# Cross attention of block one: scores from two 64-row halves of PE, the shift row laid by SP's transfers, the low key parts stacked by GpSimd

## The chip, the cores and the metric

The kernel runs on one core of one Trainium2 chip. The metric is the time of one execution on the device, in microseconds (us), less is better. The core has five engines that run side by side and wait for one another by semaphores: PE (TensorE, matrix products, with its weight loads listed apart as PEld), DVE (VectorE), ACT (ScalarE), POOL (GpSimd) and SP (SyncE, which here only issues transfers, DMAs). Products go to PSUM, of eight banks of 512 f32 columns by 128 partitions; everything else lies in SBUF, of 128 partitions.

## The reference

A chain of four attention blocks over x of 32 batches by 56 tokens by 128 channels, with a context of 1500 rows for each batch. The change is in the cross attention of block one:

```python
def _L1_xattn_ref(x, context, Wqkv, bqkv, Wos, bos, Wq, bq, Wkv, bkv, Woc, boc, W1, b1, W2, b2):
    ...
    h = _ln(x)
    q = (h @ Wq + bq).reshape(Bx, Nx, H, D)          # 16 heads of 8 channels
    kv = (context @ Wkv + bkv).reshape(Bx, Mx, 2, H, D)
    k, v = (kv[:, :, 0], kv[:, :, 1])
    a = _sdpa(q, k, v).reshape(Bx, Nx, C)            # softmax(q k / sqrt(8)) v
    x = x + (a @ Woc + boc)
```

## The kernel before, in words

The kernel goes through its stages one after the other. The stage of the change is `cross_attention` (L998), behind `tokens_l1_cross` (L926), which makes its queries. It handles one batch a step, with the engines on different batches at a time: a batch's keys are projected in one step, the maxima of its scores are sought in the next, its scores and weighted sums are made in the two after that.

What a batch goes through:

- PE projects keys (`project_k`, L1145, three products of 500 columns in f32) and values (`project_v`, L1158), ACT copies them out of PSUM (L1246, L1256, L1258).
- POOL splits the f32 keys `kf` into an f16 high part `kh` (L1101) and an f16 low part `kl` (L1103), so that scores from f16 products keep their precision.
- `piece` (L1168) makes rough scores from the high parts, 21 products of 128 by 500 in f16, and DVE takes the maximum of each (L1289). The maximum of each query is the shift of its softmax. DVE collects them (`top`, L1310), PE turns them from a column to rows (L1218), DVE copies the 7 rows of 128 to `topt` (L1300), and POOL's `lay_shift` (L1110) spreads them over rows 96 to 102 of `qs`.
- SP stacks the keys by DMA (L1066, L1070): in `ks`, for each of four groups of four heads, rows 0 to 31 and 32 to 63 hold the high part, 64 to 95 the low part, and rows 96 to 102 hold ones. `qs` holds the queries' high part, low part and high part against them (made by POOL, L1087, from `qst`), each masked to its head, and the shift at the ones. So one product of 103 rows gives the exact score less its shift.
- `score` (L1183): for each of 12 slices of 125 keys, four such products (one for a group of heads), 128 weight columns of `ks` and 224 moving columns of `qs`. They fill two PSUM banks of `stp`; ACT takes the exponential of both at once (L1235).
- `weigh` (L1200): the weighted sums, f32, on four parts of PE of 32 columns each (`tile_position=(0, q)`), three slices at a time, four times in a batch.

The order of PE's work is written out by hand in `step` (L1207 on): 12 slots of a step, in each a weighing, a projection or the turning of the shift where one is due, then `piece`, `score`, `piece`. Slots 7, 10, 1 and 4 have the weighings; the turning is in slot 11. The score of slot 2 is the first of a batch, and is where PE waits for the stacked keys, the spread queries and the shift. The score's place is always between two other products of full size.

Before the stage, `tokens_l1_cross` makes `qst` from copies of the query weights (`wqs`, three times 32 columns for each group), and ACT (L975) and DVE (L960) split it into parts. Row products on parts of PE also occur elsewhere: `norm_pe` (L452) and L1389 use four parts of 32 rows (`tile_position=(32 * c, 0)`). All transfers of SP go in the order in which it issues them, and a semaphore counts 16 for each that has landed.

## Time and profile before

| | |
|---|---|
| median of 3 runs | 2227.27 us (2222.23 to 2234.25) |
| the profiled execution | 2220.8 us, its span 2219.0 us |
| PE busy in the span | 1897.6 us (86%) |
| DVE, ACT, POOL busy | 1490.4, 1396.4, 955.3 us |
| mean granted clock of PE | 0.917 of 2.4 GHz |
| stage of the change, first score to the last | 464.7 to 1139.5 us |

The page gives sums by engine and by line; the stage is read from stretches of the span (busy time of each engine in it), from the list of who waited for whom, and from the timeline, which gives each instruction or run of like instructions with its start and length. A product's listed length holds some 0.165 us in which its results are still on their way while the next already streams: a product of 500 columns is listed with 0.37 us and the next starts 0.21 us after it. So the distance from start to start is the time that a product costs PE.

### The profile page before, as it was taken

The page shows a single profiled execution, that of the slowest core. Times are in us where ns is not written, and L with a number is a line of the kernel's source. Part 1 is how long each engine was busy: PE and PEld are TensorE (multiplying, and loading weights), DVE is VectorE, ACT ScalarE, POOL GpSimd, SP SyncE. Part 2 cuts the span into 40 slices and gives each one's busy share as a digit, 9 for nine tenths or more (in the row PEclk, how much of TensorE's full clock was granted, in tenths as well). Part 3 has the DMA queues.
Part 4 walks back from the last instruction along what each step waited for, and adds up shares of the span by engine and source line. Part 5 has one row for each costly group of instructions (what it writes and reads, how often), then busy time and mean ns, then how long its engine had stood idle before and what let it go on. Part 6 is the DMA issues. An engine that isn't in the chain of part 4 may idle for free. (4 is left out here: it accounts for less than half of the span.)

```text
span 2219.0 us, 57559 instructions
## 1 busy us (share of the span) xinstructions
PE 1897.6 (86%) x19877; PEld 1284.0 (58%) x19877; DVE 1490.4 (67%) x2708; ACT 1396.4 (63%) x2431; POOL 955.3 (43%) x1151
## 2 busy tenths in 40 slices
PE   4888676789999999999988887656899999999988
PEld 3888333256666666666653555233466666666653
DVE  3688578666666666666632332697488888888883
ACT  3787233356666666666633334433799999999963
POOL 0000064244454544545400000251688888888840
PEclk9899778799999999999988889755899999999989
DMA  7788100133332333333230997000011111111100
GB/s 210 222 257 257 17 1 0 42 78 96 90 94 83 90 90 84 98 88 90 72 103 20 272 290 222 0 0 28 29 46 52 43 42 42 42 42 42 42 1 17
DMA packets 64286, 190.38 MB, mean 86 GB/s; under 512 B 19886, under 2 KB 27294, under 8 KB 64222
## 3 DMA queue, kind: packets, MB, share of 16 engines
q1 hardware_dynamic: 59614, 164.95, 26.5%
q0 software_dynamic: 4608, 24.58, 2.8%
q8 instruction: 39, 0.64, 0.1%
q14 instruction: 25, 0.20, 0.0%
HBM read 127.13 MB, written 25.49 MB: 69 GB/s over the span
## 5 line engine op out<-in xcount | busy, mean ns | idle before, releaser
L1289 DVE TENSOR_REDUCE c_part<-c_mxp 128x1 f32<-128x500 f32 x672 | 429.0, 678 | 207.9 <-PE c_mxp L1168 207.7
L1235 ACT ACTIVATE c_e<-c_stp 125x896 f32<-125x896 f32 x384 | 349.4, 917 | 167.6 <-PE c_stp L1183 166.4
L1936 ACT ACTIVATE c_e<-c_sp,alpha 128x750 f32<-128x750 f32 x448 | 393.0, 896 | 16.9 <-PE c_sp L1881 16.9
L1168 PE MATMUL c_mxp<-c_kh,c_qb 128*128 128x500 f16 x672 | 254.4, 381 | 11.1 <-DVE c_part L1289 6.9
L1958 DVE TENSOR_SCALAR c_pt<-c_tp 125x768 bf16<-125x768 f16 x448 | 245.6, 550 | 2.1 <-PE c_tp L1894 0.8
L1894 PE MATMUL c_tp<-ident_h,c_ph 128*128 128x128 f16 x2688 | 224.3, 220 | 19.0 <-DVE c_pt L1958 15.8
L1894 PEld LDWEIGHTS c_tp<-ident_h,c_ph 128*128 128x128 f16 x2688 | 178.0, 98 | 106.1 <-DVE c_pt L1958 60.3
L1972 DVE TENSOR_SCALAR c_ph<-c_e,c_inv 128x1500 f16<-128x1500 f32 x224 | 231.2, 1032 | 0.1
L1881 PE MATMUL c_sp<-c_ki,c_qb 128*128 128x375 bf16 x896 | 218.7, 326 | 10.5 <-ACT c_e L1936 10.0
L1183 PE MATMUL c_stp<-c_qs,c_ks 103*128 103x224 f16 x1536 | 210.2, 259 | 2.5 <-ACT c_e L1235 2.5
L1183 PEld LDWEIGHTS c_stp<-c_qs,c_ks 103*128 103x128 f16 x1536 | 147.2, 98 | 72.1 <-issue 20.5
L1110 POOL TENSOR_TENSOR c_qs<-c_topt,mask_tile_ 7x896 f16<-7x896 f32 x32 | 53.8, 1681 | 293.8 <-DVE c_topt L1300 293.8
L1200 PE MATMUL c_pvp<-c_e,c_vx 125*32 125x168 f32 (+1 forms) x6144 | 173.8, 261 | 1.0 <-ACT c_e L1235 1.0
L1200 PEld LDWEIGHTS c_pvp<-c_e,c_vx 125*32 125x32 f32 x6144 | 145.1, 110 | 48.4 <-issue 33.6
L1947 ACT ACTIVATE c_rounded<-c_pp,round,rdelta 128x500 f32<-128x500 f32 (+1 forms) x192 | 149.6, 779 | 36.3 <-PE c_pp L1870 22.3
L1824 POOL TENSOR_SCALAR c_clamped<-c_rounded 128x500 f32<-128x500 f32 (+1 forms) x192 | 136.9, 713 | 36.4 <-ACT c_rounded L1947 16.3
L1833 POOL TENSOR_SCALAR c_ki<-c_clamped 128x500 bf16<-128x500 f32 x96 | 113.4, 1181 | 17.3 <-issue 15.8
L1881 PEld LDWEIGHTS c_sp<-c_ki,c_qb 128*128 128x128 bf16 x896 | 69.0, 98 | 83.6 <-ACT c_e L1936 46.7
L1103 POOL TENSOR_TENSOR c_kl<-c_kf,c_kh 128x500 f16<-128x500 f32 x96 | 109.1, 1136 | 8.0
L1870 PE MATMUL c_pp<-a2wv,c_ct 128*125 128x128 f32 x768 | 107.6, 284 | 2.6 <-ACT c_rounded L1947 2.6
L1865 PE MATMUL c_pp<-c_ct,a2wk 128*128 128x500 f32 x192 | 105.4, 632 | 4.9 <-POOL c_ph L1815 2.9
L1145 PE MATMUL c_pp<-c_ct,wkv 128*128 128x500 f32 x192 | 104.5, 627 | 4.8 <-PEq L87 2.2
(276 smaller groups left out, 3534.7 us busy)
## 6 DMA issues: line engine op xcount, KB each, us to landing
c_ct<-ctx_turned SPq DMA_DIRECT2D x64, 750.0 KB
ctx_turned<-l_ct POOLq DMA_DIRECT2D x32, 750.0 KB, 7.6
c_ks<-c_kh SPq DMA_DIRECT2D x256, 93.8 KB
f_ct<-ctx_turned SPq DMA_DIRECT2D x32, 750.0 KB
l_cn<-in_ctx SPq DMA_DIRECT2D x32, 672.0 KB
f_cn<-in_ctx SPq DMA_DIRECT2D x32, 672.0 KB
c_ks<-c_kl SPq DMA_DIRECT2D x128, 93.8 KB
l_cn<-in_ctx SPq DMA_DIRECT2D x32, 78.0 KB
```

What stands on the lines that cost most here:

```text
L1168: pe.matmul(mxp[:, (PIECES * p + s) % 2, 0:500], qh[p][:, 128 * (s // 3):128 * (s // 3) + 128], kh[p][:, 500 * (s % 3):500 * (s % 3) + 500 ...
L1183: last = pe.matmul(stp[:, 2 * (j % 2) + g // 2, 224 * (g % 2):224 * (g % 2) + 224], ks[p][:, g, KP * j:KP * j + 128], qs[p][:, 224 * g:224 ...
L1200: last = pe.matmul(pvp[q:q + 32, c:c + width], vx[p][:, j, g, :], e[:, j % (2 * GROUP), NQ * h:NQ * h + width], start=(j == 0 and g < 4), ...
L1235: act.activation(e[:, j % (2 * GROUP), :].rearrange("p (a c) -> p a c", a=2), stp[0:KP, 2 * (j % 2):2 * (j % 2) + 2, 0:448], ACT.Exp, scal ...
L1289: dve.reduce_max(part[:, s // 3, s % 3:s % 3 + 1], mxp[:, (PIECES * p + s) % 2, 0:500], axis=AX.X).then_inc(piece_max, 1)
L1824: pool.tensor_scalar(clamped[k % 2][0:rows, 0:width], rounded[k % 2][0:rows, 0:width], ROUND + 127.0, ROUND - 128.0, ALU.min, ALU.max).the ...
L1881: last = pe.matmul(sp_[:, 2 * h + k, 0:375], qb[p][:, 128 * t:128 * t + 128], ki[p][:, HALF * h + 375 * k:HALF * h + 375 * k + 375], start ...
L1894: last = pe.transpose(tp[:, h, 128 * k:128 * k + 128], ph[t % E_BUFFERS][:, KP * j:KP * j + 128], m.ident_h[:, :])
L1936: act.activation(e[t % E_BUFFERS][:, HALF * h:HALF * h + HALF] .rearrange("p (k c) -> p k c", k=2), sp_[:, 2 * h:2 * h + 2, 0:375], ACT.Ex ...
L1947: act.activation(rounded[k % 2][0:rows, 0:width], pp[0:rows, 0:width], ACT.Identity, bias=m.round[0:rows, 0:1], scale=m.rdelta[0:rows, d:d ...
L1958: dve.tensor_scalar(pt[p][:, 6 * h:6 * h + 6, 128 * t:128 * t + 128], tp[0:KP, h, 0:6 * 128].rearrange("p (j c) -> p j c", j=6), HALF_ROUN ...
L1972: dve.tensor_scalar(ph[t % E_BUFFERS][:, 0:NK], e[t % E_BUFFERS][:, :], inv[:, t:t + 1], HALF_ROUND, ALU.mult, ALU.add).then_inc(p_ready, 1)
```

## The change

The score's product of 103 rows becomes two of 64 rows, on the upper and the lower half of PE's rows, each with half of the heads and 112 moving columns; the two halves write different PSUM banks. Within a half, rows 0 to 15 and 16 to 31 hold the high part of two heads' keys, row 32 is a row of ones for the shift (rows 33 to 47 are ones as well, against zeros), and rows 48 to 63 hold the low part. `ks` is filled by 16 transfers of 16 rows from SP and 8 of 16 rows from POOL (before: 12 of 32 rows from SP). The shift goes to rows 32 and 96 of `qs` by 8 small transfers from SP in place of POOL's instruction L1110. POOL's four instructions L1087 become one on 128 rows by 448 columns. `qst` is laid out for it, with weights from 12 small loads in place of 6 and products of 128 columns in place of 96. The memsets of ones cover 128 partitions, and SP and POOL wait for them before the first stacking.

```diff
-    for t in range(3):
-        loads.append((m.wqs[:, :, 32 * t:32 * t + 32], w["L1_xattn_Wq"].rearrange("c (g r) -> c g r", g=4)))
-        loads.append((m.bqs[32 * t:32 * t + 32, :], w["L1_xattn_bq"].rearrange("(g r) -> r g", g=4)))
+    for half in range(2):
+        wide, narrow = w["L1_xattn_Wq"][:, 64 * half:64 * half + 64], w["L1_xattn_bq"][64 * half:64 * half + 64]
+        for at in (0, 16, 48):
+            a = 64 * half + at
+            loads.append((m.wqs[:, :, a:a + 16], wide.rearrange("c (g r) -> c g r", g=4)))
+            loads.append((m.bqs[a:a + 16, :], narrow.rearrange("(g r) -> r g", g=4)))
...
-                        dve.scalar_tensor_tensor(out=m.qst[32:64, g, cols(c)], in0=bank[32:64, 4 + i % 4, 0:CH],
-                                                 scalar=m.bqs[32:64, g:g + 1], in1=m.qst[32:64, g, cols(c)],
+                        dve.scalar_tensor_tensor(out=m.qst[:, g, cols(c)], in0=bank[:, 4 + i % 4, 0:CH],
+                                                 scalar=m.bqs[:, g:g + 1], in1=m.qst[:, g, cols(c)],
                                                  op0=ALU.add, op1=ALU.subtract).then_inc(qs_low, 1)
...
-                        act.activation(m.qst[:, g, cols(c)], bank[0:96, 4 + i % 4, 0:CH], ACT.Identity,
-                                       bias=m.bqs[:, g:g + 1]).then_inc(qs_high, 1)
+                        act.activation(m.qst[:, g, cols(c)], bank[:, 4 + i % 4, 0:CH], ACT.Identity,
+                                       bias=m.bqm[:, g:g + 1], scale=m.mask_rows[:, 2:3]).then_inc(qs_high, 1)
...
-        ks = pair("ks", [96 + NT, 4, W], F16)
+        ks = pair("ks", [128, 4, W], F16)
-        qs = pair("qs", [96 + NT, HQ], F16)
+        qs = pair("qs", [128, HQ // 2], F16)
...
+                        sp.wait_ge(qs_spread, n - 1)
+                        sp.wait_ge(top_copied, n - 1)
+                        for t in range(NT):
+                            for c in (0, 64):
+                                at = 128 * t + c
+                                row, at = (32, at) if at < HQ // 2 else (96, at - HQ // 2)
+                                if t == NT // 2:
+                                    sp.dma_start(qs[p][row:row + 1, at:at + 64], topt[t:t + 1, c:c + 64]
+                                                 ).then_inc(shift_sent[p], 16)
+                                elif c == 0:
+                                    sp.dma_start(qs[p][row:row + 1, at:at + 128], topt[t:t + 1, :]
+                                                 ).then_inc(shift_sent[p], 16)
                     if live(1):
                         r = 1 - p
+                        if not live(2):
+                            sp.wait_ge(ones_set, 2)
                         if live(3):
                             wait_apart(sp, scored, NJ * (n - 2), beat)
                         sp.wait_ge(k_high, 3 * n)
-                        for t in range(2):
-                            for g in range(4):
-                                sp.dma_start(ks[r][32 * t:32 * t + 32, g, 0:NK], kh[r][32 * g:32 * g + 32, 0:NK]
-                                             ).then_inc(stacked[r], 16)
-                        sp.wait_ge(k_low, 3 * n)
-                        for g in range(4):
-                            sp.dma_start(ks[r][64:96, g, 0:NK], kl[r][32 * g:32 * g + 32, 0:NK]
-                                         ).then_inc(stacked[r], 16)
-                sweep(sp, step, 1)
+                        for at in (0, 16):
+                            for half in (0, 64):
+                                for g in range(4):
+                                    sp.dma_start(ks[r][half + at:half + at + 16, g, 0:NK],
+                                                 kh[r][half + 16 * g:half + 16 * g + 16, 0:NK]
+                                                 ).then_inc(stacked[r], 16)
+                sweep(sp, step, 2)
...
-                    for g in range(4):
-                        last = pool.tensor_tensor(
-                            qs[p][0:96, 4 * NQ * g:4 * NQ * (g + 1)].rearrange("p (h q) -> p h q", h=4),
-                            m.qst[:, g, tokens(a)].rearrange("p (o q) -> p o q", o=1).to_broadcast([96, 4, NQ]),
-                            m.mask_quad[0:96, :].rearrange("p (h o) -> p h o", o=1).to_broadcast([96, 4, NQ]),
-                            ALU.mult)
-                    last.then_inc(qs_spread, 1)
+                    pool.tensor_tensor(qs[p][:, :].rearrange("p (g h q) -> p g h q", g=4, h=2),
+                                       m.qst[:, :, tokens(a)].rearrange("p g (o q) -> p g o q", o=1)
+                                       .to_broadcast([128, 4, 2, NQ]),
+                                       m.mask_rows[:, 0:2].rearrange("p (o h u) -> p o h u", o=1, u=1)
+                                       .to_broadcast([128, 4, 2, NQ]), ALU.mult).then_inc(qs_spread, 1)
+
+                def stack_low(a, p, live):
+
+                    if not live(2):
+                        pool.wait_ge(ones_set, 2)
+                    wait_apart(pool, k_low, 3 * a + 3, beat)
+                    for half in (0, 64):
+                        for g in range(4):
+                            pool.dma_start(ks[p][half + 48:half + 64, g, 0:NK],
+                                           kl[p][half + 16 * g:half + 16 * g + 16, 0:NK]).then_inc(low_stacked[p], 16)
 
...
-                def lay_shift(a, p, more):
-
-                    if more:
-                        pool.wait_ge(k_low, 3 * a + 6)
-                    pool.wait_ge(top_copied, a + 1)
-                    pool.tensor_tensor(qs[p][96:96 + NT, :].rearrange("p (t c) -> p t c", t=NT),
-                                       topt[:, :].rearrange("p (o c) -> p o c", o=1).to_broadcast([NT, NT, 128]),
-                                       m.mask_tile[:, :].rearrange("p (t o) -> p t o", o=1)
-                                       .to_broadcast([NT, NT, 128]), ALU.mult).then_inc(shift_laid, 1)
-
                 def step(n, p, live):
                     if live(1):
                         spread_queries(n - 1, 1 - p, live)
+                        stack_low(n - 1, 1 - p, live)
                     if live(0):
                         if live(2):
-                            pool.wait_ge(shift_laid, n - 1)
...
-                        pe.wait_ge(stacked[p], transfers(a, p, 12))
+                        pe.wait_ge(stacked[p], transfers(a, p, 16))
+                        pe.wait_ge(low_stacked[p], transfers(a, p, 8))
                         pe.wait_ge(qs_spread, a + 1)
-                        pe.wait_ge(shift_laid, a + 1)
+                        pe.wait_ge(shift_sent[p], transfers(a, p, 8))
                     if j >= 2 or not first:
                         pe.wait_ge(exped, NJ * a + j - 1)
                     for g in range(4):
-                        last = pe.matmul(stp[:, 2 * (j % 2) + g // 2, 224 * (g % 2):224 * (g % 2) + 224],
-                                         ks[p][:, g, KP * j:KP * j + 128], qs[p][:, 224 * g:224 * g + 224],
-                                         start=True, stop=True)
+                        for half in range(2):
+                            r = 64 * half
+                            last = pe.matmul(stp[:, 2 * (j % 2) + half, 112 * g:112 * g + 112],
+                                             ks[p][r:r + 64, g, KP * j:KP * j + 128],
+                                             qs[p][r:r + 64, 112 * g:112 * g + 112], start=True, stop=True,
+                                             tile_position=(r, 0))
...
-                    dve.memset(ks[p][96:96 + NT, :, :], 1.0).then_inc(ones_set, 1)
+                    dve.memset(ks[p][:, :, :], 1.0).then_inc(ones_set, 1)
...
-                                dve.wait_ge(shift_laid, n - 1)
+                                dve.wait_ge(shift_sent[p], transfers(n - 2, p, 8))
```

## Rows read from the trace of the kernel before

**Rows 1.** Stretch: us, busy (count) of PE, PEld, DVE, ACT, POOL; PEclk, DMA share, GB/s.

```profile
464.70:1139.50 674.80, 651.15 (x9232) 460.30 (x9231) 446.67 (x802) 467.21 (x660) 319.38 (x361) 1.00 0.32 85
```

**Rows 2.** Who waited for whom between 500 and 1100 us: total, times, longest.

```profile
DVE c_part L1289 <- PE c_mxp L1168: 183.3, 280, 0.9
...
PE c_pp L1218 <- DVE c_top L1310: 16.7, 28, 0.6
```

**Rows 3.** Timeline of PE in one batch: start, us, what, count, idle before.

```profile
950.42 0.37 PE L1168 MATMUL c_mxp<-c_kh,c_qb 128*128 128x500 f16 x1
950.63 0.55 PE L1183 MATMUL c_stp<-c_qs,c_ks 103*128 103x224 f16 x4
951.02 0.38 PE L1168 MATMUL c_mxp<-c_kh,c_qb 128*128 128x500 f16 x1
951.33 1.36 PE L1200 MATMUL c_pvp<-c_e,c_vx 125*32 125x168 f32 x48
...
953.98 0.28 PE L1218 MATMUL c_pp<-ident_,c_top 128*7 128x128 f32 x1 [0.60 <-DVE c_top L1310]
954.09 0.55 PE L1183 MATMUL c_stp<-c_qs,c_ks 103*128 103x224 f16 x4
...
957.28 0.38 PE L1168 MATMUL c_mxp<-c_kh,c_qb 128*128 128x500 f16 x1
957.49 1.00 PE L1145 MATMUL c_pp<-c_ct,wkv 128*128 128x500 f32 x2
...
958.54 0.55 PE L1183 MATMUL c_stp<-c_qs,c_ks 103*128 103x224 f16 x4
```

**Rows 4.** PE's timeline, window 952.44 to 952.70, around the end of a weighing.

```profile
952.14 0.55 PE L1200 MATMUL c_pvp<-c_e,c_vx 125*32 125x168 f32 x13
952.62 0.38 PE L1168 MATMUL c_mxp<-c_kh,c_qb 128*128 128x500 f16 x1
```

**Rows 5.** As rows 1, line 1389 alone: products of 32 rows on four parts.

```profile
1151.40:1154.80 3.40, 3.38 (x16) 1.30 (x16) 0.50 1.04 373
```

**Rows 6.** As rows 1, line 445 alone: products of 128 rows, same columns.

```profile
250.20:256.40 6.20, 6.08 (x8) 2.52 (x8) 0.53 0.24 2
```

**Rows 7.** PE's timeline at 1701.6: six transposes, a weight load each.

```profile
1701.68 0.50 PE L1894 MATMUL c_tp<-ident_h,c_ph 128*128 128x128 f16 x6
```

**Rows 8.** Weight loads of the scores by line: busy us, mean ns, idle before.

```profile
L1183 PEld LDWEIGHTS c_stp<-c_qs,c_ks 103*128 103x128 f16 x1343 | 129.1, 98 | 61.8 <-issue 18.0 <-ACT c_e L1235 9.0
```

**Rows 9.** Timeline of all engines around the shift and the next batch's keys.

```profile
954.29 0.28 DVE L1300 COPY c_topt<-c_pp 7x128 f32<-7x128 f32 x1 [0.37 <-PE c_pp L1218]
...
954.72 1.68 POOL L1110 TENSOR_TENSOR c_qs<-c_topt,mask_tile_ 7x896 f16<-7x896 f32 x1 [9.08 <-DVE c_topt L1300]
...
957.54 4.94 SPq L1066 DMA_DIRECT2D c_ks<-c_kh  x8
957.61 2.11 POOL L1087 TENSOR_TENSOR c_qs<-qst,mask_quad_ 96x224 f16<-96x224 f32 x4 [1.21 <-PE c_stp L1183]
...
962.52 2.50 SPq L1070 DMA_DIRECT2D c_ks<-c_kl  x4
...
965.82 1.13 POOL L1103 TENSOR_TENSOR c_kl<-c_kf,c_kh 128x500 f16<-128x500 f32 x1
```

**Rows 10.** Timeline of SP's queue from 237.7 us: small transfers.

```profile
237.74 0.30 SPq L503 DMA_DIRECT2D wocb<-in_L_xattn_Woc  x1
238.08 0.29 SPq L503 DMA_DIRECT2D bvb<-in_L_xattn_bkv  x1
```

**Rows 11.** DMA busy tenths in 40 slices of 0.325 us, 957 to 970 us.

```profile
DMA  0000083929191929393939383848000000000000
```

**Rows 12.** GpSimd's DMA instructions, line 314: min/median/max ns, first and last start.

```profile
L314 POOL DMA_DIRECT2D ctx_turned<-l_ct x32: 533/533/749, 29.7 to 220.5; - x32
```

**Rows 13.** Timeline of DVE and PE at the stage's start.

```profile
436.29 5.07 DVE L1270 MEMSET c_ks<- 7x6016 f16 x1 [1.20 <-issue]
...
465.14 0.77 PE L1183 MATMUL c_stp<-c_qs,c_ks 103*128 103x224 f16 x3
```

More of the change, by code:

```diff
@@ L209, in _ @@
             def _(pool):
-                for t in (m.woca, m.wocb, m.bva, m.bvb):
+                for t in (m.woca, m.wocb, m.bva, m.bvb, m.bqs):
                     pool.memset(t[:, :], 0.0)
+                pool.memset(m.wqs[:, :, :], 0.0)
                 pool.memset(m.mean[:, :], 1.0 / D)
@@ L965, in _ @@
             def _(act):
+                act.wait_ge(small, 7)
                 norm_act(act, m, n2, bank)
@@ L1076, in _ @@
                 for p in range(2):
-                    pool.memset(ks[p][0:96, :, NK:W], 0.0).then_inc(set_once, 1)
                     pool.memset(kh[p][:, NK:W], 0.0).then_inc(set_once, 1)
@@ L2215, in constants @@
     spread[:, 1] = (l[:, None] == 12 + g) & (l < DH)
+    block = r % 64 // 16
+    mask_rows = np.zeros((128, 3), np.float32)
+    for h in range(2):
+        mask_rows[:, h] = (r % 16 // DH == h) & (block != 2)
+    mask_rows[:, 2] = block == 1
     key, of_head = np.arange(2 * NQ), np.arange(D) // DH
```

30 lines of the change are left out of this document (16 added, 14 removed).

## The prediction, on record before the run

> **What bounds the kernel now.** I read the busy time by stretches first. Between the first score and the last, PE is busy 651.15 of 674.80 us at the full clock (1.00), DVE 446.67, ACT 467.21, POOL 319.38 [rows 1]. The list of waits agrees: over 600 us DVE sat idle for PE's products 280 times, 183.3 us in all, while PE itself has one wait for another engine in each batch, 0.60 us for the maxima, 16.7 us in 28 batches [rows 2]. 28 batches in 600 us make 21.4 us a batch. So PE sets the pace, and whatever its queue gains or loses in a batch comes back some 32 times. The timeline shows how close its products stand [rows 3]: a product of 500 columns starts at 950.42, four score products at 950.63, the next product at 951.02. So a score costs PE 0.39 us, 4.7 us in a batch.
>
> **The score products.** With both halves streaming side by side, each half has 4 x 112 columns where the whole had 4 x 224. 0.39 us falls to some 0.19 us, worth 12 x 0.19 = 2.3 us in a batch, if nothing is added. Three things bear on it.
>
> Do row parts run side by side? Line 1389 has eight f32 products of 448 columns, 16 instructions, on four parts of 32 rows; they took 3.40 us at the half clock (0.50) [rows 5]. Line 445 has four such products on all rows, 8 instructions, and took 6.08 us at nearly the same clock (0.53) [rows 6]. Twice the work in 0.56 of the time: the parts overlap fully, so I take two halves as overlapping fully too. Their weight loads overlapped as well: 16 in 1.30 us of busy PEld [rows 5].
>
> Can the weights keep up? Each product of 112 columns brings its own load of 128 weight columns. Six transposes, each with such a load and 128 moving columns, took 0.50 us, of which the first 0.22 us is latency: 0.056 us each [rows 7]. A load is listed with 98 ns [rows 8], but most of that is latency too. So a half needs 4 x 0.047 to 4 x 0.056 us, 0.19 to 0.22; I take 0.20.
>
> What does the change of shape cost? The weighing uses PE in four parts of 32 columns. Before it the product of 500 columns starts at 951.02 and would free PE at 951.23 (its 0.21 us of streaming, as above), but the weighing starts at 951.33: 0.10 us [rows 3]. At its end, the last of its products ends at 952.14 + 0.55 = 952.69; less 0.165 us of latency its streaming ends at 952.52, and the next full product starts at 952.62: again 0.10 us [rows 4]. That is not the change of type: f16 is followed by f32 at 957.28 and 957.49 with the bare 0.21 us between [rows 3]. The trace has no switch between full and row shape with work waiting on both sides, so its cost lies between nothing and, by these rows, 0.10 us; I take 0.10, since entering and leaving the parts cost the same and f32 or f16 made no difference. Each of the 12 scores stands between two full products, so it pays twice: 0.10 + 0.01 for the first weights + 0.20 + 0.10 = 0.41 to 0.42 us against 0.39. **The switches eat the overlap**: +0.03 us x 12 = +0.36 us in a batch, 11.5 us in 32. Bounds: 0.19 us a score without any switch cost (-2.3 us in a batch), 0.45 with slow weights and both switches (+0.7).
>
> The Trainium skill (TensorEngine Tiling (Array Packing), Key Properties) says that a change of the tiling mode drains the engine; the 0.10 us in rows 3 and 4 agree for column parts, and nothing before shows it for rows. Its table of speedups on the same page gives "up to 2x" for a contraction of at most 64; by that alone the scores would save 2.3 us in a batch, 74 us in all.
>
> **The shift.** Today `topt` is ready at 954.29 + 0.28 = 954.57, POOL takes 954.72 to 956.40 [rows 9], and the score that needs it starts at 958.54 [rows 3]: 2.1 us of slack, cost zero. Now SP issues 8 transfers and they must land. SP is free then: its last instructions before are the load of the context, long issued, and it waits for this very event. Behind its wait stand the 16 stackings, which today start at 957.54 after their own wait for the scores [rows 9]; nothing is needed from them before the next batch. Small transfers were issued 0.34 us apart [rows 10], the stackings 4.94/8 = 0.62 us apart. From issue to landing: the stackings are issued from 957.54 and traffic starts at slice 5 of the DMA line, 958.6; the last is issued at some 964.4 and traffic ends in slice 29, 966.4 [rows 9, 11]. So 1.1 us to the start and 1.9 us to the end; a small one should land between 1.3 and 1.9 us after its issue. The eighth lands at 954.7 + 7 x 0.34 + 1.3 = 958.4 at best, at 954.7 + 7 x 0.62 + 1.9 = 960.9 at worst. PE needs it at 958.54 + 0.19 for three longer scores and a switch, 958.7. The wait is 0 to 2.2 us; small transfers are nearer to the pitch of rows 10, so I take 0.42 us and 1.6 us: 959.2, a wait of **0.5 us**. It holds up PE's whole queue (the next pieces, the key projections), so all of it counts: 0.5 x 31 = 15.5 us. DVE, starved by it, has slack; the one wait of PE for the maxima stays.
>
> **POOL.** It loses 1.68 us and some 1.1 us (one instruction of 448 columns in place of 2.11 us for four of 224), and gets 8 DMA instructions. The first stage shows one alone at 0.53 to 0.75 us [rows 12]. 8 x 0.57 = 4.6 us, between the spread and the next split of keys. That split now ends at 965.82 + 1.13 = 966.95 [rows 9] and moves to some 970.4; it is needed for the first piece after 954.09 + 21.4 + 0.4 = 975.9. The cover is 9 us; it would be gone at 1.25 us per instruction. Cost zero. The low parts land by some 967 and are needed at 980.
>
> **SP and DMA.** 16 x 0.62 = 9.9 us in place of 7.4, issued from 957.5 to 967.5, needed at 980; the next context load comes at 972. Same bytes. Cost zero.
>
> **Ahead of the stage.** The second memset ends at 436.29 + 5.07 = 441.4; SP now waits for it 3.8 us longer, but the first score starts only at 465.14 [rows 13]. The six more weight loads lie beside PE's work in an earlier stage. DVE, ACT and PE have as many instructions in making `qst`. Zero.
>
> **Sum.** 2220.8 us for the profiled execution + 11.5 + 15.5 = 2247.8. The median of the runs shown lies 6.5 us above that execution, so I forecast 2254 us.
>
> **Rivals.**
> - *No cost of switching to rows.* The scores save 12 x 0.18 = 2.1 us in a batch. But three of them lie between the maxima and the shift's need, which then comes 0.6 us earlier, so the wait grows to 1.1 us: 1.0 us in a batch gained, 32 us, about 2195 us; 2160 if the shift comes in time. For it: rows 5 has no gap between its parts. Against it: every entry and exit seen costs 0.10 us. It decides at 0.08 us per switch: below that the score itself gains, and below 0.06 it outweighs the wait for the shift.
> - *The shift comes in time.* Then only the switches count: 2220.8 + 11.5 + 6.5 = 2239 us. For it: the lower landing estimate.
> - *The halves don't overlap, or their weights come too slowly.* 8 x 0.05 + 0.21 = 0.61 us a score, +2.7 us in a batch, no wait for the shift: +86 us, 2313 us. Against it: rows 5 and 6, though at the half clock and in f32.
> - *Transfers or POOL's instructions slower than taken.* The wait at the upper bound, 2.2 us: +54 us more, 2305 us.
>
> **How the numbers follow.** Forecast (2240 to 2285 us) 0.50; no switch cost, or little of it 0.15; shift in time 0.14; no overlap 0.11; slow transfers 0.10. The predicted time is 2254 us. The range 2215 to 2310 leaves out most of the first rival and part of the last two. 0.5% (11 us) is about what a measurement can tell from no change: below 2216 us 0.14, between 2216 and 2238 us 0.17, above 0.69.
>
> **What would show it.** In the profile after, the two products of 500 columns around a score start 0.62 to 0.63 us apart (the 0.21 us of the first, then 0.41 to 0.42); 0.41 says that switching is free, over 0.72 that the halves take turns. The first weight load of a score starts 0.10 us after the stream before has ended. The waits list PE's scores behind SP's transfers of `qs`, once in a batch, 0.5 us each; none says in time. The stage then lasts 27 us more. DVE's idle time for PE grows; the clock stays at 1.00. I am wrong if the scores' starts are closer, if PE waits for POOL, or if another stage moves.

## The result, and the profile after

| | median, us | lowest to highest, us | runs |
|---|---|---|---|
| before | 2224.75 | 2220.31 to 2234.25 | 4 |
| after | 2306.86 | 2301.48 to 2318.10 | 4 |

The kernel is slower: ratio 1.037, 95% interval 1.0317 to 1.0422, some 82 us. The profiled execution of after is the slowest of its four: 2318.1 us, span 2316.2, 97.2 more than the span of before.

The stage by stretches, columns as in [rows 1]: the whole stage, its beginning, and its steady middle (740 to 1190 us, in which the batches take nearly the same time and the clock is 1.00).

```profile
467.80:1235.20 767.40, 660.63 (x10767) 404.40 (x10767) 454.50 (x801) 457.76 (x659) 347.82 (x479) 0.97 0.32 76
467.80:650.00 182.20, 157.18 (x2391) 93.16 (x2395) 104.91 (x182) 104.72 (x151) 83.13 (x115) 0.93 0.33 77
740.00:1190.00 450.00, 389.97 (x6384) 239.31 (x6383) 278.44 (x490) 273.64 (x397) 221.53 (x304) 1.00 0.34 80
```

The stage is 767.40 us long, where [rows 1] has 674.80: 92.6 of the 97.2 us. PE's busy time has grown by 9.5 us only, so PE stands idle. The clock column is new too: 0.97 where it was 1.00, and 0.93 up to 650 us.

Who PE waited for, over the stage, and in the last line over its steady middle, 740 to 1190 us (total, times, longest):

```profile
PE c_stp L1202 <- DMA c_qs<-c_topt: 81.5, 32, 4.8
PE c_pp L1238 <- DVE c_top L1330: 21.0, 31, 0.7
...
PE c_stp L1202 <- DMA c_qs<-c_topt: 45.5, 19, 2.6
```

One wait has come in, in each of 32 batches: the first score (line 1202) behind the shift's transfers, 45.5/19 = 2.4 us each in the middle. The wait for the maxima, PE's one wait for another engine in [rows 2], is nearly as it was: 21.0/31 = 0.68 us against 0.60.

The timeline of PE in one batch of the middle:

```profile
949.98 0.38 PE L1184 MATMUL c_mxp<-c_kh,c_qb 128*128 128x500 f16 x1
950.29 0.37 PE L1202 MATMUL c_stp<-c_qs,c_ks 64*128 64x112 f16 x8
...
952.13 0.38 PE L1184 MATMUL c_mxp<-c_kh,c_qb 128*128 128x500 f16 x1 [0.22 <-issue]
952.45 0.37 PE L1202 MATMUL c_stp<-c_qs,c_ks 64*128 64x112 f16 x8
952.75 0.38 PE L1184 MATMUL c_mxp<-c_kh,c_qb 128*128 128x500 f16 x1
...
956.04 0.37 PE L1184 MATMUL c_mxp<-c_kh,c_qb 128*128 128x500 f16 x1
958.61 0.37 PE L1202 MATMUL c_stp<-c_qs,c_ks 64*128 64x112 f16 x8 [2.20 <-DMA c_qs<-c_topt]
```

Read the distances of starts. Piece 952.13, score 952.45, piece 952.75: 0.62 us from piece to piece, where [rows 3] has 0.60. From 949.98 to 950.29 is 0.31 us, of which 0.21 us is the piece's streaming: entering the halves costs 0.10 us. Then 952.75 - 952.45 = 0.30 us: 0.20 us for eight products on two halves and 0.10 us to leave them. How the 0.30 us divide is the prediction's estimate here; the kernel with scores in pairs, below, shows it. The last piece ahead of the shift's score streams until 956.25. The score starts at 958.61, with 2.20 us of idle time ahead of it that the row puts down to the transfers.

The same batch on the other engines, DVE's copy of the maxima first:

```profile
951.65 0.28 DVE L1320 CAST c_topt<-c_pp 7x128 f16<-7x128 f32 x1 [0.37 <-PE c_pp L1238]
...
952.01 1.79 SPq L1077 DMA_DIRECT2D c_qs<-c_topt  x3
...
953.85 1.22 SPq L1074 DMA_DIRECT2D c_qs<-c_topt  x2
...
955.11 1.85 SPq L1077 DMA_DIRECT2D c_qs<-c_topt  x3
...
956.13 3.92 POOL L1118 DMA_DIRECT2D c_ks<-c_kl  x8
...
957.17 10.09 SPq L1089 DMA_DIRECT2D c_ks<-c_kh  x16
```

The eight shift transfers (lines 1077 and 1074) start 0.08 us after the copy's end at 951.93 and are issued every 0.61 to 0.63 us: 3 in 1.79 us, 2 in 1.22, 3 in 1.85. The last issue begins near 956.34; PE starts 2.3 us later, so it has landed by some 2.2 us after its start. (The profile's own time from issue to landing has a median of 1.7 us over these transfers, 3.1 at most.) [rows 9] shows GpSimd doing the same work in one instruction of 1.68 us. What followed in the queues gave no trouble: GpSimd's eight stackings took 3.92 us, SP's sixteen 10.09 us, and the list of waits has neither as a releaser of PE.

To compare kernels I use the period of a batch: the starts of DVE's copies of the maxima between 750 and 1100 us, the last less the first, divided by one less than their count. The rows give count, min/median/max ns, first and last start; the second is of before.

```profile
L1320 DVE CAST c_topt<-c_pp x15: 278/279/279, 760.8 to 1095.0; 7x128 f16<-7x128 f32 x15
```

```profile
L1300 DVE COPY c_topt<-c_pp x16: 277/279/279, 761.0 to 1083.0; 7x128 f32<-7x128 f32 x16
```

(1095.0 - 760.8)/14 = 23.87 us, against (1083.0 - 761.0)/15 = 21.47 us.

### The profile page after: what moved, and what is told of

Read it like the earlier page. It is cut to its first block and busy times, and to the rows that moved or that the text cites. A ratio compares the mean times of both kernels' runs of the same rounds, so it can differ in the third digit from the quotient of the medians.

```text
span 2316.2 us, 61141 instructions
## 1 busy us (share of the span) xinstructions
PE 1895.0 (82%) x21413; PEld 1224.6 (53%) x21413; DVE 1500.8 (65%) x2709; ACT 1390.3 (60%) x2431; POOL 991.0 (43%) x1279
## 5 line engine op out<-in xcount | busy, mean ns | idle before, releaser
L1309 DVE TENSOR_REDUCE c_part<-c_mxp 128x1 f32<-128x500 f32 x672 | 437.3, 678 | 288.3 <-PE c_mxp L1184 287.9
L1184 PE MATMUL c_mxp<-c_kh,c_qb 128*128 128x500 f16 x672 | 261.0, 391 | 11.6 <-DVE c_part L1309 6.5
L1901 PE MATMUL c_sp<-c_ki,c_qb 128*128 128x375 bf16 x896 | 218.6, 326 | 10.5 <-ACT c_e L1956 10.0
L1202 PE MATMUL c_stp<-c_qs,c_ks 64*128 64x112 f16 x3072 | 144.6, 215 | 83.7 <-DMA c_qs<-c_topt 81.5
L1202 PEld LDWEIGHTS c_stp<-c_qs,c_ks 64*128 64x128 f16 x3072 | 83.9, 96 | 215.3 <-issue 163.8
L1105 POOL TENSOR_TENSOR c_qs<-qst,mask_rows_ 128x448 f16<-128x448 f32 (+1 forms) x32 | 29.9, 934 | 356.6 <-PE c_stp L1202 356.6
L1118 POOL DMA_DIRECT2D c_ks<-c_kl x256 | 125.5, 497 | 7.6 <-issue 5.0
L1184 PEld LDWEIGHTS c_mxp<-c_kh,c_qb 128*128 128x128 f16 x672 | 65.0, 97 | 85.5 <-DVE c_part L1309 27.6
## 6 DMA issues: line engine op xcount, KB each, us to landing
c_ks<-c_kh SPq DMA_DIRECT2D x512, 46.9 KB
c_ks<-c_kl POOLq DMA_DIRECT2D x256, 46.9 KB
```

Of the source, the lines that this page charges most:

```text
L1184: pe.matmul(mxp[:, (PIECES * p + s) % 2, 0:500], qh[p][:, 128 * (s // 3):128 * (s // 3) + 128], kh[p][:, 500 * (s % 3):500 * (s % 3) + 500 ...
L1202: last = pe.matmul(stp[:, 2 * (j % 2) + half, 112 * g:112 * g + 112], ks[p][r:r + 64, g, KP * j:KP * j + 128], qs[p][r:r + 64, 112 * g:112 ...
L1309: dve.reduce_max(part[:, s // 3, s % 3:s % 3 + 1], mxp[:, (PIECES * p + s) % 2, 0:500], axis=AX.X).then_inc(piece_max, 1)
L1901: last = pe.matmul(sp_[:, 2 * h + k, 0:375], qb[p][:, 128 * t:128 * t + 128], ki[p][:, HALF * h + 375 * k:HALF * h + 375 * k + 375], start ...
```

## The experiments

| kernel | median, us | ratio to before, 95% interval | period, us |
|---|---|---|---|
| before | see below | 1 | 21.47 |
| after | 2306.9 | 1.037 (1.0317 to 1.0422) | 23.87 |
| after without the shift | 2222.3 | 1.0006 (0.999 to 1.0022) | 21.63 |
| before with halves only | 2222.5 | 1.0009 (0.9993 to 1.0025) | 21.63 |
| before with the shift by SP | 2270.5 | 1.0226 (1.0198 to 1.0253) | 22.84 |
| shift in four transfers | 2223.8 | 1.001 (0.999 to 1.0029) | 21.65 |
| eight transfers out of HBM | 2222.7 | 1.001 (0.9989 to 1.0031) | 21.64 |
| shift in two queues | 2245.3 | 1.0091 (1.0064 to 1.0118) | 21.94 |
| low stackings back on SP | 2227.6 | 1.0021 (1.0003 to 1.0038) | 21.64 |
| scores in pairs | 2212.0 | 0.9932 (0.99 to 0.9964) | 21.06 |
| pairs, key eviction earlier | 2198.4 | 0.9879 (0.9854 to 0.9904) | 20.70 |
| wait filled | 2300.3 | 1.0344 (1.031 to 1.0378) | 23.90 |

The periods are each read from one profiled execution. The kernel before had a median of 2221.35, 2223.06 and 2222.08 us beside the first four, the next four and the last two of them.

### After without the shift

```diff
-                    if live(2):
-                        sp.wait_ge(qs_spread, n - 1)
-                        sp.wait_ge(top_copied, n - 1)
-                        ...  the eight sp.dma_start(qs[p][row:row + 1, ...], topt[...])
...
-                        pe.wait_ge(shift_sent[p], transfers(a, p, 8))
```

> The kernel after without SP's eight transfers of the shift and the waits on them: the exponentials are taken without the maxima (this part of the computation is left out; the maxima are still made). Theory A (the loss is the wait for the shift, 81.5 us in the profile after, plus the switches of shape, 12 x 0.03 us in a batch): 11 to 15 us over the kernel before, ratio 1.005, and the two products of 500 columns around a score stay 0.62 us apart. Rival B (the loss is in the 24 stacking transfers or in POOL's eight DMA instructions): it stays 50 us or more over before, with PE waiting for another transfer or for POOL.

2222.3 us. The stage, columns as before:

```profile
467.20:1144.00 676.80, 649.15 (x10764) 398.44 (x10765) 452.70 (x802) 455.63 (x660) 347.11 (x479) 1.00 0.35 85
```

676.80 us, 2.0 more than [rows 1], at the clock 1.00. So the 82 us sit in the shift, and the row halves with all their switches cost next to nothing: the kernel is at 1.0006 of before. The period is 0.16 us longer than before's: 5 us in 31 batches, which the interval of the ratio cannot tell from none. The 11 to 15 us that I expected did not come.

### Before with halves only

```diff
-                        last = pe.matmul(stp[...], ks[p][:, g, KP * j:KP * j + 128],
-                                         qs[p][:, 224 * g:224 * g + 224], start=True, stop=True)
+                        for half in range(2):
+                            r, end = (0, 64) if half == 0 else (64, 96 + NT)
+                            at = 224 * g + 112 * half
+                            last = pe.matmul(stp[...112 columns...], ks[p][r:end, g, KP * j:KP * j + 128],
+                                             qs[p][r:end, at:at + 112], start=True, stop=True,
+                                             tile_position=(r, 0))
```

The kernel before with its scores cut into products on two halves of the rows. Each half takes 112 columns of its own rows' products alone, so that part of each score's sum is left out.

> The kernel before with one part of the change: each score product of 103 rows by 224 columns is replaced by two, of rows 0 to 63 and 64 to 102, on the two halves of PE's rows, 112 columns each, in two banks. The halves are not added up, so the scores are left incomplete; shift and stacking are as before. Theory A: switches cost what the overlap gains, 0.41 to 0.42 us a score against 0.39, +8 to +14 us, ratio 1.004 to 1.006. Rival C (row halves are worth what they promise, and only the shift spoils it): -60 to -70 us. Rival D (halves cost more than seen): over +30 us.

2222.5 us. PE's timeline around one score:

```profile
950.60 0.38 PE L1168 MATMUL c_mxp<-c_kh,c_qb 128*128 128x500 f16 x1
950.92 0.37 PE L1186 MATMUL c_stp<-c_qs,c_ks 64*128 64x112 f16 x8
951.22 0.38 PE L1168 MATMUL c_mxp<-c_kh,c_qb 128*128 128x500 f16 x1
```

The same 0.62 us from piece to piece, and the period of 21.63 us, without any other part of the change. No saving of 60 to 70 us, and no loss of 80; nor the 8 to 14 us of theory A, since the kernel is only 1.1 us over before (interval of the ratio 0.9993 to 1.0025). A score of two halves takes 0.41 us, of which 0.20 us is the entry and the exit. Halving the streaming and paying the switch cancel, to 0.02 us.

### Before with the shift by SP

```diff
+                        for t in range(NT):
+                            sp.dma_start(qs[p][96 + t:97 + t, 128 * t:128 * t + 128], topt[t:t + 1, :]
+                                         ).then_inc(shift_sent[p], 16)
...
-                def lay_shift(a, p, more):
...
-                        pe.wait_ge(shift_laid, a + 1)
+                        pe.wait_ge(shift_sent[p], transfers(a, p, NT))
```

> The kernel before with one other part of the change: the shift goes to its seven rows by seven transfers of 256 bytes from SP in place of POOL's instruction; full-row scores. Theory A: transfers between SBUF places are issued 0.62 us apart and land 1.7 to 2.0 us after issue, so the seventh lands 5.6 to 5.9 us after the copy of the maxima; PE needs it after 4.0 to 4.3 us: a wait of 1.5 to 1.9 us in each of 31 batches, +45 to +60 us, ratio 1.02 to 1.027. Rival E (the small transfers are slow only beside POOL's own DMAs, or because of the 24 stackings): pitch near 0.34 us, no wait, +0 to +5 us.

2270.5 us, 49 more than the kernel before beside it. SP's queue, and PE's waits over 600 us:

```profile
944.44 4.31 SPq L1065 DMA_DIRECT2D c_qs<-c_topt  x7
...
PE c_stp L1178 <- DMA c_qs<-c_topt: 38.8, 26, 2.8
```

Full-row products, GpSimd with its old work but for the shift, and yet a wait of 38.8/26 = 1.5 us in a batch: seven transfers of 256 B in 4.31 us, 0.62 us each. The shift's way through SP's queue is enough to slow the kernel; the halves are not needed for it.

### The shift in four transfers

```diff
-                        ...  eight transfers, one for each row of topt and each half
+                        for row, at, t, c, tiles, wide in ((32, 0, 0, 0, 3, 128), (32, 384, 3, 0, 1, 64),
+                                                           (96, 0, 3, 64, 1, 64), (96, 64, 4, 0, 3, 128)):
+                            sp.dma_start(qs[p][row:row + 1, at:at + tiles * wide]
+                                         .rearrange("o (t c) -> o t c", t=tiles),
+                                         topt[t:t + tiles, c:c + wide]).then_inc(shift_sent[p], 16)
```

> The kernel after with the shift sent by four transfers in place of eight (three tiles of 128 in one, twice; the middle tile in two halves); the result is the same. Theory A (a transfer's issue costs 0.6 us whatever it carries): the fourth lands 0.13 + 3 x 0.62 + 1.9 = 3.9 us after the copy, in time or nearly; 12 to 25 us over before, ratio 1.005 to 1.011. Rival F (the landing or the number of pieces in a transfer counts, not the number of transfers): the wait stays over 1.5 us, over 55 us above before.

2223.8 us: next to nothing is left of the 82. SP's queue, and PE's waits from 500 to 1100 us:

```profile
960.21 2.71 SPq L1071 DMA_DIRECT2D c_qs<-c_topt  x4
...
PE c_stp L1198 <- DMA c_qs<-c_topt: 0.8, 1, 0.8
```

Four transfers of the same bytes take 2.71 us to issue, 0.68 each, so three rows in one cost as good as one; they are done 2.3 us earlier, and the wait is gone but for once in these 600 us, 0.8 us. I had expected 12 to 25 us over before, since I still held the switches at 11.5.

### Eight transfers out of HBM

```diff
-                        ... sp.dma_start(qs[p][row:row + 1, at:at + 128], topt[t:t + 1, :]
+                        ... sp.dma_start(qs[p][row:row + 1, at:at + 128], m.shift_source[t:t + 1, :]
```

> The kernel after, its eight shift transfers on SP kept in number, size, order and destination, but read from a constant in HBM in place of the copied maxima in SBUF (the true shift is left out of the result's scores). Theory A (a transfer on SP's queue costs 0.62 to 0.63 us when it reads SBUF and 0.34 us when it reads HBM; the pitch is set by where it reads): eight issues take 2.7 us in place of 5.0, the last is issued near 954.7 by the time of the kernel after, lands before 957, and PE's wait of 2.2 to 2.6 us falls to 0 to 0.5 us a batch: 2225 to 2245 us. Rival G (the pitch belongs to transfers that write SBUF on waiting for an engine, whatever they read): 0.6 us each stays and with it 2290 to 2310 us. Rival H (landing of small transfers from HBM is longer, 2.0 us and more, and gives back half): 2245 to 2275 us.

The source is a constant of zeros in HBM, so the scores are taken without the maxima as their shift.

2222.7 us, just under the 2225 to 2245 of theory A. SP's queue in one batch:

```profile
957.09 0.83 SPq L1077 DMA_DIRECT2D c_qs<-in_shift_source  x3
...
958.55 0.85 SPq L1077 DMA_DIRECT2D c_qs<-in_shift_source  x3
959.86 10.01 SPq L1089 DMA_DIRECT2D c_ks<-c_kh  x16
```

Eight issues in 2.31 us (957.09 to 959.40), 0.29 us each, where the small transfers of [rows 10] start 0.34 us apart. The sixteen stackings right behind, which read SBUF, take 10.01/16 = 0.63. So with size, number, order and destination the same, the source alone takes the pitch from 0.62 to 0.29 us, and the time the pitch costs is all of the loss: with 0.29 us the wait is not in the list of waits from 500 to 1100 us at all. It doesn't follow that every transfer out of HBM is cheap to issue. SP's queue in before, shortly ahead of [rows 10], and at the load of a batch's context:

```profile
233.74 0.60 SPq L503 DMA_DIRECT2D bqs<-in_L_xattn_bq  x1
...
950.77 0.34 SPq L1052 DMA_DIRECT2D c_ct<-ctx_turned  x1
```

Both read HBM. The small bias, which its load takes in another order (`rearrange("(g r) -> r g")`), costs 0.60 us, and 750 KB of context only 0.34. So size doesn't set the cost, and the source isn't all that does; what the order of reading adds was not tried.

### The shift in two queues

```diff
+                def send_shift(a, p):
+                    wait_apart(pool, qs_spread, a + 1, beat)
+                    wait_apart(pool, top_copied, a + 1, beat)
+                    for at, t, c in ((0, 3, 64), (64, 4, 0), (192, 5, 0), (320, 6, 0)):
+                        pool.dma_start(qs[p][96:97, at:at + 128 - c], topt[t:t + 1, c:128]
+                                       ).then_inc(pool_sent[p], 16)
```

> The kernel after with the eight shift transfers in two queues: four on SP's (the first half of the positions), four on GpSimd's, each engine waiting for the copied maxima. Theory A (the price is the issue by one engine, one after the other): SP needs 4 x 0.62 = 2.5 us and GpSimd 4 x 0.49 = 2.0 us side by side, the last lands some 4.5 us after the copy in place of 6.7, before PE reaches its first score; no wait on the shift, 2222 to 2235 us. Rival I (the transfers share one rate behind both queues, so that eight still take 5 us): 2290 to 2310 us. Rival J (GpSimd's wait for the maxima holds back its spreading of the queries and of the keys, and PE waits for these instead): 2240 to 2280 us with GpSimd named as releaser of PE's or SP's idle time.

2245.3 us: over A's 2222 to 2235, and inside J's 2240 to 2280, but PE's waits name neither GpSimd nor its work, as J would have it. Both queues in one batch, and PE's waits from 500 to 1100 us:

```profile
948.74 1.80 SPq L1079 DMA_DIRECT2D c_qs<-c_topt  x3
...
949.26 2.01 POOL L1128 DMA_DIRECT2D c_qs<-c_topt  x4 [7.21 <-DVE c_topt L1334]
...
950.58 0.59 SPq L1076 DMA_DIRECT2D c_qs<-c_topt  x1
...
PE c_stp L1215 <- DMA c_qs<-c_topt: 10.4, 5, 2.9
```

The queues do run side by side: four from SP by 951.17, four from GpSimd by 951.27, 0.60 and 0.50 us each. There is no shared rate. In most batches PE doesn't wait; in five of these 600 us it does, for 2.1 us on average. In one of these the copy ends at 682.05 and GpSimd starts only at 685.29:

```profile
681.77 0.28 DVE L1334 CAST c_topt<-c_pp 7x128 f16<-7x128 f32 x1 [0.37 <-PE c_pp L1251]
...
685.29 2.01 POOL L1128 DMA_DIRECT2D c_qs<-c_topt  x4 [9.84 <-issue]
```

What held it those 3.2 us the trace doesn't say ("issue"). Theory A holds for the transfers, not for the kernel's time, which is 22 us over before. The profiled execution is one of the faster, 2240.05 us, and 14.2 over that of the four transfers. By the last copy of the maxima it is 12.0 us behind (1145.6 against 1133.6): 4.5 at the first copy already (465.4 against 460.9), where these kernels differ by as much without a cause that I know, and 7.5 over the 31 batches, in which the late ones lie. The rest, up to the median's 22 us, no profile shows.

### Low stackings back on SP

```diff
+                        sp.wait_ge(k_low, 3 * n)
+                        for half in (0, 64):
+                            for g in range(4):
+                                sp.dma_start(ks[r][half + 48:half + 64, g, 0:NK],
+                                             kl[r][half + 16 * g:half + 16 * g + 16, 0:NK]).then_inc(...)
...
-                def stack_low(a, p, live):
```

On top of the four transfers.

> The kernel with the shift in four transfers, and the eight low stackings moved back from GpSimd's queue to SP's, behind its sixteen high ones. Theory A (the move to GpSimd's queue hides nothing and costs nothing: SP's stacking has some 10 us of slack before the next scores need it): SP's stacking grows from 10 us to 15 us and ends some 9 us before the first score of the next batch; 2220 to 2230 us, ratio to the kernel before 0.998 to 1.004. Rival K (SP's queue was full: the stacking pushes the context's load or the next shift late, and PE waits 0.3 us or more a batch): 2235 to 2260 us.

2227.6 us. SP's queue:

```profile
954.49 5.03 SPq L1091 DMA_DIRECT2D c_ks<-c_kl  x8
959.82 0.34 SPq L1059 DMA_DIRECT2D c_ct<-ctx_turned  x1
963.13 2.70 SPq L1071 DMA_DIRECT2D c_qs<-c_topt  x4
```

The stackings end at 959.52, the context's load goes out at 959.82, and SP then stands idle until 963.13. The period is that of the four transfers, 21.64 us against 21.65. So the move to GpSimd's queue neither hides nor costs anything measurable: the two ratios' intervals overlap.

### Scores in pairs

```diff
-                        if s >= SCORE_AT and live(2):
-                            score(n - 2, p, s - SCORE_AT, not live(3))
+                        if s % 2 == 0 and s >= SCORE_AT and live(2):
+                            for j in (s - SCORE_AT, s - SCORE_AT + 1):
+                                score(n - 2, p, j, not live(3))
```

Also on top of the four transfers; ACT's exponentials are paired alike.

> The kernel with the shift in four transfers, its twelve scores of a batch issued in six pairs (at every second piece), so that PE changes between row halves and full rows six times in place of twelve at the scores. Theory A (a change of 0.095 us each way on PE's path): the six pairs save 6 x 0.19 = 1.1 us a batch, 35 us over the stage, if PE's rate alone sets the batch: 2188 to 2200 us, ratio 0.985 to 0.99. Rival L (the changes lie under PE's waits for other engines, the batch being set by the ring PE, VectorE, ScalarE): no change, 2218 to 2230 us. Rival M (pairs come in bursts, PE waits for the maxima's or exponentials' buffers after each): 2230 to 2260 us, with PE's idle time at a score or a piece put down to VectorE or ScalarE.

2212.0 us: faster than before (0.9932, interval 0.99 to 0.9964), but none of the three ranges has it, and the period falls by half of the 1.1 us that theory A expected. PE's timeline, and its waits over the stage:

```profile
956.09 0.39 PE L1180 MATMUL c_mxp<-c_kh,c_qb 128*128 128x500 f16 x1
956.40 0.57 PE L1198 MATMUL c_stp<-c_qs,c_ks 64*128 64x112 f16 x16
956.90 0.39 PE L1180 MATMUL c_mxp<-c_kh,c_qb 128*128 128x500 f16 x1
...
959.24 1.14 PE L1170 MATMUL c_pp<-wkv,c_ct 128*125 128x128 f32 x8 [0.69 <-ACT c_kf L1264]
...
PE c_pp L1170 <- ACT c_kf L1264: 20.6, 30, 0.7
```

Piece to piece over a pair is 0.81 us, 0.60 for two scores against 2 x 0.41: 0.22 us saved per pair, 1.3 us in a batch. From the pair's start to the next piece it is 0.50 us, where eight products had 0.30: eight products more cost 0.20 us, so 0.10 us is left for leaving the halves. The period fell by 21.65 - 21.06 = 0.59. The rest is in the new wait: the value projection (line 1170) waits 0.69 us for the eviction of the last keys, which now stands behind two exponentials.

### Pairs, key eviction earlier

```diff
                             for i in (j - SCORE_AT, j - SCORE_AT + 1):
                                 exponentials(n - 2, i, live(3))
+                                if live(0) and j + 1 == K_SLOTS[2] and i == j - SCORE_AT:
+                                    keys(2)
```

> The kernel with paired scores, with one order changed on ScalarE: the eviction of a batch's third key projection stands between the two exponentials of its pair, not behind both. In the paired kernel PE's first value projection waits 0.69 us for that eviction (958.50 us, behind 1.73 us of exponentials), 30 times, 20.6 us in all. Theory N (that wait is where half of the gain of the pairs went, since nothing else is late there): the eviction starts 0.7 us earlier, PE's wait goes, 15 to 20 us less than the paired kernel: 2192 to 2198 us, ratio to the kernel before 0.985 to 0.989. Rival O (the exponential pushed back by 0.7 us holds the next pair of scores, or VectorE's maxima set the pace behind it): 2205 to 2215 us, as the paired kernel, with PE's idle time moved to the scores or pieces.

2198.4 us, ratio 0.9879 (0.9854 to 0.9904), 14 us less than the pairs alone. Theory N has the place right and the size a little high: it expected 15 to 20 us and the end of the wait, and the wait only halved. The two ratios' intervals just touch, so that the step from the pairs rests on the period and the wait more than on the medians. PE's waits:

```profile
PE c_pp L1170 <- ACT c_kf L1262: 10.5, 30, 0.4
```

The wait fell from 20.6 to 10.5 us, 0.35 us a batch, and the period by 0.36 us; no other wait of PE grew by more than 1.2 us over the stage. This kernel does the whole computation, and beats both before and after.

### The wait filled

```diff
+                        if s == SCORE_AT and live(1) and live(2):
+                            f = 2 * s + 1
+                            pe.wait_ge(piece_max, PIECES * (n - 1) + f - 1)
+                            for _ in range(10):
+                                pe.matmul(mxp[...], qh[1 - p][...], kh[1 - p][...], start=True, stop=True)
```

> The kernel after, in which PE fills the wait for the shift: ten more products of 500 columns (2.1 us at the full clock, a repeat of the next piece, nothing that the result needs) stand ahead of the first score of each batch. Theory P (the half-clock stretches of the first ten batches of this stage follow PE's waits of 2 us and more; they, and the late batches of 25 to 27 us that come with them, go once PE stays busy, while the shift itself still ends last at 23.9 us a batch): the granted clock of the stage rises from 0.97 to 1.00, and the kernel takes 2288 to 2300 us, 7 to 18 us less than after. Rival Q (the low clock has another cause, for example the stage's entry at 467 us): the clock stays at 0.97 and the time at 2303 to 2312 us. Rival R (the filling outlasts the wait in steady batches and adds to it): 2312 us and more.

2300.3 us, at the upper end of P's 2288 to 2300. First what there is to explain. In after, the first score of the fourth batch, with the wait ahead of it, and the stretch around it:

```profile
545.84 0.56 PE L1202 MATMUL c_stp<-c_qs,c_ks 64*128 64x112 f16 x8 [3.79 <-DMA c_qs<-c_topt]
...
543.40:550.20 6.80, 4.36 (x25) 1.74 (x29) 1.49 (x3) 2.17 (x3) 6.28 (x10) 0.57 0.53 104
```

PE had stood idle for 3.79 us; the granted clock, 1.00 from 536 to 543, is 0.57 from 543.4 to 550.2, most of it at the lower level of 1.2 GHz, and the score with it: listed with 0.56 us, where eight products have 0.37 at the full clock. With the wait filled, the stage's beginning:

```profile
467.80:560.00 92.20, 86.55 (x1273) 51.22 (x1271) 55.33 (x96) 55.76 (x82) 40.32 (x54) 0.99 0.34 81
560.00:650.00 90.00, 86.29 (x1315) 51.65 (x1315) 55.60 (x98) 54.36 (x78) 46.62 (x64) 1.00 0.33 77
```

0.99 and 1.00, where after has 0.93 up to 650 us, and PE's waits for the shift add up to 15.9 us over the stage in place of 81.5. So the fall of the clock did follow from PE's idleness. Over the whole stage, the 32 copies of the maxima:

```profile
L1327 DVE CAST c_topt<-c_pp x32: 277/278/279, 462.3 to 1205.0; 7x128 f16<-7x128 f32 x32
```

```profile
L1320 DVE CAST c_topt<-c_pp x32: 278/279/279, 461.3 to 1215.6; 7x128 f16<-7x128 f32 x32
```

(1205.0 - 462.3)/31 = 23.96 us a batch against (1215.6 - 461.3)/31 = 24.33: 11.6 us less over the stage of these two executions. The medians differ by 6.5 us, and their ratios' intervals overlap, so the size is open: the clock is shown, its price lies between nothing and some 12 us. In steady batches nothing changed (23.90 and 23.87): there the shift ends last, whether PE is busy meanwhile or not.

## Why the prediction was wrong

I forecast 2254 us, 27 of it for the change; it took 2306.9, with 82 us for the change. The direction was right, and so was what bounds the kernel; the size was not. The shares, in the profiled executions: over 31 periods after is 31 x (24.33 - 21.43) = 90 us longer, 21.43 being before's mean over the same 31, (1123.9 - 459.7)/31. Of these the switches are 31 x 0.16 = 5, the shift's steady wait 31 x (23.87 - 21.63) = 69, and what single batches lose beyond that 31 x (24.33 - 23.87) = 14; the sum is 88.

**PE sets the pace: right.** What its queue loses in a batch comes back in the period, if not to the last tenth: a wait of 1.5 us made the period 1.37 us longer (the shift by SP), one of 2.4 us 2.24 (after against after without the shift), and with the two kernels of pairs waits and periods agree to 0.02 us.

**The overlap and the switches: right in kind and size, the sum a little high.** Entering and leaving row halves costs 0.10 us each, as rows 3 and 4 gave for column parts, and eight products stream in 0.20. The score takes 0.41 us and not 0.39, as said. But I rounded up to +0.03 us and multiplied by 12: 0.36 us in a batch. Piece to piece grew by 0.02 (0.24 us in a batch) and the period by 0.16; what absorbs the other 0.08 I didn't trace. The term of 11.5 us measured 5, and no more than 5 us by the interval of the kernel without the shift (1.0022). The Trainium skill (TensorEngine Tiling (Array Packing), Key Properties) has the drain without a number; the runs agree with it for row halves, and the "up to 2x" of its Theoretical Speedup came for the streaming alone (0.20 us in place of 0.39) and not for groups of eight products that each pay the switch twice. The pairs, which pay it half as often, are where the saving begins.

**The shift: this is the step that failed.** The mechanism, the place and PE's whole queue behind it were as written, the size was not. I took a pitch of 0.42 us because "small transfers are nearer to the pitch of rows 10", and a landing of 1.6 us. Small they are, but rows 10's transfers read HBM; the stackings of rows 9, at 0.62 us, read SBUF as the shift does. That was the row to go by: the issues took 0.62 us each, and the wait is 2.4 us a batch where the sum has 0.5, or 69 us over the stage in place of 15.5. Counted from the end of the copy: seven pitches took 4.35 us in place of 2.94 (+1.4), the landing 2.2 in place of 1.6 (+0.6), the start 0.1. The landing of 2.2 lies outside my bounds of 1.3 to 1.9 as well. Together the eighth lands 6.6 us after the copy's end, where I had 959.2 - 954.57 = 4.6. PE was ready 4.4 us after it, where I had 4.1. So the wait is 2.2 us in this batch, and the rival at the upper bound, "slow transfers", with one chance in ten, has the mechanism that happened. That its 2305 us came within 2 us of 2306.9 is partly luck: it has 11.5 us of switches where some 5 were paid, nothing for the 14 us of single batches, and by its own terms the sum is 2307 us (2254 + 31 x 1.7). The rival of free switches is out by the 0.10 us each way; its threshold, put at 0.08 us, is 0.09 by its own numbers (0.39 - 0.21 us, halved). The kernel with four transfers and the one reading HBM show it from two sides: fewer issues, or cheaper ones, and the wait goes, with the change otherwise whole.

Between two bounds I chose by size of the transfer, where the two rows differed in source as well. Nothing in the trace of before said that size was what counted, and two of its rows spoke against it: 750 KB of context issued in 0.34 us, and a small bias, out of HBM too, in 0.60 (both under the eight transfers out of HBM).

**The clock stays at 1.00: wrong.** Half-clock stretches came in the first third of the stage, behind waits such as the 3.79 us shown. Filling the wait brought the clock back. The length of the wait isn't what tells the batches apart. Two first scores of after with the waits ahead of them, and the stretches behind them:

```profile
670.66 0.56 PE L1202 MATMUL c_stp<-c_qs,c_ks 64*128 64x112 f16 x8 [2.19 <-DMA c_qs<-c_topt]
...
696.16 0.37 PE L1202 MATMUL c_stp<-c_qs,c_ks 64*128 64x112 f16 x8 [2.60 <-DMA c_qs<-c_topt]
...
670.60:677.00 6.40, 6.34 (x80) 3.37 (x81) 2.83 (x5) 2.92 (x4) 6.22 (x9) 0.73 0.56 119
696.10:703.00 6.90, 6.84 (x97) 3.92 (x98) 4.81 (x10) 4.73 (x6) 6.70 (x9) 1.00 0.49 110
```

Behind 2.19 us the clock was 0.73, behind 2.60 us 1.00, and it stayed so in the middle, at waits of 2.2 to 2.6 us. What decides it is open. Some of the longest waits have a slow issue in them; the issues of the fourth and fifth transfer, count, min/median/max ns, first and last start:

```profile
L1074 SPq DMA_DIRECT2D c_qs<-c_topt x64: 588/589/1622, 463.5 to 1218.4; - x64
```

The median is 0.59 us, the longest 1.62. What made single ones that long the trace doesn't give.

**GpSimd, SP's stackings, the stage's entry: right.** GpSimd's eight took 3.92 us (I had 4.6) and nobody waited; SP's sixteen 10.09 us (9.9). The first score is at 467.8 against 465.14 [rows 13], but it lies anywhere between 463.9 and 471.2 in the kernels above, so I put nothing down to the change.

## What to carry to other kernels

Price a DMA's issue by a row with the same source memory, the same queue and a like order of reading, not by one of the same size; count the issues that stand between an event and the work that waits for it, and fold them into fewer, since three rows in one cost as good as one. Row parts of PE pay 0.10 us on the way in and 0.10 us on the way out: group the products of one shape before asking what the parts save. And where one edit frees PE, look at once at the order on the engine that evicts for it: half of the pairs' gain lay under one eviction in the wrong place.

## What the runs showed of the hardware that I had not expected

- On SP's queue a transfer out of SBUF takes 0.59 to 0.63 us of issue, for 256 B and for 46.9 KB alike; out of HBM 0.29 us for the same 256 B into the same row, but 0.34 us for 750 KB of context and 0.60 us for a small bias that is read in another order. On GpSimd's queue 0.49 to 0.50 us out of SBUF.
- SP's and GpSimd's issues run side by side at these rates. The Trainium skill (DMA: Bandwidth & Descriptors, Issuing engines are not separate DMA queues) says that starting DMAs on several engines saves only the time on the sequencer, "usually small relative to the DMA itself". Here it is not small: 8 x 0.62 us of issue against some 2 us of landing.
- Behind a wait of 3.79 us the granted clock was 0.57 over 6.8 us; behind the waits of 2.2 to 2.6 us in the steady middle it stayed at 1.00. The wait's length doesn't tell the two apart: behind 2.19 us at 670.66 the clock was 0.73, behind 2.60 us at 696.16 it was 1.00. What does was not tried.
